# Cross attention on one core: the value mixes of two pairs of heads back to back in every second step, and four buffers of exponentials

## The chip, the cores and the metric

One NeuronCore of a Trainium2 chip runs one program: a decoder of four layers. The metric is the device time of one execution in microseconds (us), lower is better. TensorE (PE) multiplies; its weight loads (PEld) are separate instructions that run beside the matmuls. VectorE (DVE), ScalarE (ACT) and GpSimd (POOL) do the element work, SyncE (SP) issues the DMAs. Engines run their own instruction streams in order and wait for each other by semaphores.

## What is computed

The input x is 32 batches of 56 tokens with 128 features, the context is 32 batches of 1500 rows of 128. Each of four layers adds a self attention, a mixing with the context, and a feed forward part. In layers 1, 2 and 3 the mixing is a cross attention with 16 heads of 8 features:

```
Q = (query @ Wq + bq).reshape(B, Sq, H, D).transpose(0, 2, 1, 3)
K = (key @ Wk + bk).reshape(B, Sk, H, D).transpose(0, 2, 1, 3)
V = (value @ Wv + bv).reshape(B, Sk, H, D).transpose(0, 2, 1, 3)
scores = jnp.einsum('bhqd,bhkd->bhqk', Q, K) / jnp.sqrt(jnp.float32(D))
attn = jax.nn.softmax(scores, axis=-1)
out = jnp.einsum('bhqk,bhkd->bhqd', attn, V)
out = out.transpose(0, 2, 1, 3).reshape(B, Sq, E)
return out @ Wo + bo
```

Here query is the normalised x (56 rows a batch), key and value are both the context (1500 rows a batch).

## The kernel before

`cross_attention(chip, layer, scale)` is called three times. A call goes over the 32 batches, one batch to a *pass*; `all_passes` (L799) writes out the passes -2, -1, 0, then a hardware loop over seven groups of four passes, then the last four. Two heads make a *pair*: there are PR = 8 pairs a batch, and a pass has eight *steps*, one for each pair. Every engine has a `one_pass` of its own that fixes the order of its work by hand; semaphores tie them together.

What a pair needs, in the order in which it goes through the engines:

- `scores` (L907, matmuls L912): three matmuls, each 112 rows (two heads of 56 queries) by 500 keys, into the PSUM banks 0, 1 and 2. They run LEAD = 7 steps ahead of the rest. Bank n waits until VectorE has reduced bank n of the pair before (`topped`).
- `row_tops` (L1071, L1074): VectorE takes the largest score of each row, one reduction a bank. After four pairs, in step 4 and step 0, `split_tops` (L1076, five small operations, L1081 to L1089) splits the maxima in three bfloat16 parts. `turn_tops` (L918, L920) turns them on TensorE in steps 3 and 6; `place_first` (L1093) and `place_others` (L1097) put them beside the queries, so that the next product comes out with the maximum already taken off.
- `scores_by_key` (L922, L931): twelve matmuls give the same scores with the keys on the partitions, into the banks 3 to 5. They wait until ScalarE has emptied these banks of the pair before (`exp_done`).
- `exponentials` (L1014, L1016): one ScalarE instruction writes the exponentials of a pair to `probs_t`, of which there are two buffers.
- `mix_values` (L935, L943): the value mix, twelve fp32 products of 112 columns with 32 columns of weights (24 in the trace, since an fp32 product appears as two), on four column tiles in turn, added up in the bank MIX. It waits for the exponential of its pair. After four pairs `keep_mixed` (L1019, L1021) copies the bank away; `fold` (L948, L957) in step 3 of the next pass adds the four tiles up, and `keep_mix` (L1100) divides.

Beside these the pass makes the keys of the batch after next (`make_keys`, L891, steps 0, 1 and 2), which ScalarE copies (L1007), POOL splits (L1059 to L1065), and SP stacks by DMA; and the values of the next batch (`make_values`, L904, steps 4, 5 and 7; copy L1011).

TensorE's order in step s of a pass is: `scores_by_key` of pair s; keys, values, fold or turned tops where the step has them; `scores` of the pair seven steps ahead; `mix_values` of the pair s - 1. In step 0 that is pair 7 of the batch before.

Of the kernel before, what the change touches and what calls it, by code (L numbers as in the profile page):

```python
# [17 lines left out]
KC = 125  # L18
NC_ = NK // KC
# [732 lines left out]
PR = HX // 2  # L752
RW = 2 * S
# [8 lines left out]
VC = P // 32  # L762
VR = NC_ // VC
# [3 lines left out]
def cross_attention(chip, layer, scale):  # L767
# [9 lines left out]
    nc, ps, xn, x = chip.nc, chip.ps, chip.xn, chip.x  # L777
# [13 lines left out]
    TURNED, MIX, TURNS = 3, 6, 7  # L791
    KEY_STEPS, TURN_STEP, VALUE_STEPS, NEXT_TURN_STEP = (0, 1, 2), 3, (4, 5, 7), 6

    def wait(engine, semaphore, value):

        if not isinstance(value, int) or value > 0:
            engine.wait_ge(semaphore, value)
# [11 lines left out]
    def has(i):  # L809

        return not isinstance(i, int) or 0 <= i < B

    with ExitStack() as own:
        def sbuf(name, shape, dtype=F32):
            return own.enter_context(nc.sbuf_tensor(tag + name, shape, dtype))
# [12 lines left out]
        keys = [sbuf("keys%d" % u, [P, PR, NK], BF16) for u in range(2)]  # L828
        queries = [sbuf("queries%d" % u, [P, PR, RW], BF16) for u in range(2)]
        values = [sbuf("values%d" % u, [KC, NC_, VW]) for u in range(2)]  # L830
        probs_t = [sbuf("probs_t%d" % u, [KC, NC_, RW]) for u in range(2)]
        bank_top = sbuf("bank_top", [P, PR, NB_])
        top, top_left, top_parts = sbuf("top", [P, HP_]), sbuf("top_left", [P, HP_]), sbuf("top_parts", [P, 32], BF16)
        quarters = [sbuf("quarters%d" % u, [P, PR, 2, S]) for u in range(2)]
# [47 lines left out]
        def _(pe):  # L882
            def make_keys(i, o, n):
                if n == 0:
                    pe.wait_ge(ctx_landed[o % ROUND], 16 * ((i - o % ROUND) // ROUND) + 16 if isinstance(i, int) else 16 * ((i - o) // ROUND + o // ROUND) + 16)
                    if isinstance(i, int):
                        wait(pe, k_kept, NB_ * i)
                    wait(pe, v_kept, VR * (i - 1))
                else:
                    pe.wait_ge(k_kept, NB_ * i + n)  # L890
                nc.tensor.matmul(ps[:, TURNS, 0:KB], wk[:], ctx_t[o % ROUND][:, KB * n:KB * n + KB], start=True, stop=True).then_inc(k_done, 1)  # L891
# [30 lines left out]
            def scores_by_key(i, o, p):  # L922
                if p % HP_ == 0:
                    pe.wait_ge(first_placed, 2 * i + p // HP_ + 1)
                    if isinstance(i, int) and i == 0:
                        pe.wait_ge(both_filled, 16)
                if p % HP_ == 1:
                    pe.wait_ge(tops_placed, 2 * i + p // HP_ + 1)
                wait(pe, exp_done, PR * i + p)
                for c in range(NC_):  # L930
                    mm = nc.tensor.matmul(ps[0:KC, TURNED + c // VC, RW * (c % VC):RW * (c % VC) + RW],  # L931
                                          keys[o % 2][:, p, KC * c:KC * c + KC], queries[o % 2][:, p, :], start=True, stop=True)
                mm.then_inc(turned_done, 1)

            def mix_values(i, o, p):  # L935
                pe.wait_ge(exp_done, PR * i + p + 1)
                if p % HP_ == 0:
                    wait(pe, mixed_kept, 2 * i + p // HP_)
                if p == 0:
                    pe.wait_ge(v_kept, VR * i + VR)  # L940
                for c in range(NC_):
                    g = c % 4
                    mm = nc.tensor.matmul(ps[32 * g:32 * g + 32, MIX, RW * (p % HP_):RW * (p % HP_) + RW], values[o % 2][:, c, (PF + 1) * p:(PF + 1) * p + 32],  # L943
                                          probs_t[p % 2][:, c, :], start=(c < 4), stop=(c >= NC_ - 4))
                if p % HP_ == HP_ - 1:
                    mm.then_inc(mixed, 1)

# [19 lines left out]
            def one_pass(i, o):  # L967
                for step in range(PR):
                    if has(i):
                        scores_by_key(i, o, step)  # L970
                    if step in KEY_STEPS and has(i + 2):
                        make_keys(i + 2, o + 2, KEY_STEPS.index(step))
                    if step == TURN_STEP:
                        if has(i + 2):
                            pe.wait_ge(k_kept, NB_ * (i + 2) + NB_)
                        elif has(i + 1) or has(i):
                            pe.wait_ge(v_kept, VR * (i + 1))
                        if has(i - 1):
                            fold(i - 1, o - 1)
                        if has(i):  # L980
                            turn_tops(i, 1)
                    if step in VALUE_STEPS and has(i + 1):
                        if step == VALUE_STEPS[0] and has(i):
                            pe.wait_ge(first_placed, 2 * i + 2)
                            wait(pe, mix_kept, i)
                        make_values(i + 1, o + 1, VALUE_STEPS.index(step))
                    if step == NEXT_TURN_STEP and has(i + 1):
                        pe.wait_ge(v_kept, VR * (i + 1) + 2)
                        turn_tops(i + 1, 0)
                    ahead, pair = divmod(step + LEAD, PR)  # L990
                    if has(i + ahead):
                        scores(i + ahead, o + ahead, pair)
                    back, pair = divmod(step - 1, PR)
                    if has(i + back):
                        mix_values(i + back, o + back, pair)
            all_passes(pe, one_pass)
            for c in range(CH):
                pe.wait_ge(biased, c + 1)
                nc.tensor.matmul(ps[:, c, 0:CT], wo[:], mix[:, CB * c:CB * c + CB, :].rearrange("p b s -> p (b s)"),
                                 start=True, stop=True).then_inc(projected, 1)  # L1000

        @block.scalar
        def _(act):
            def keep_keys(i, n):
                act.wait_ge(k_done, NB_ * i + n + 1)
                wait(act, k_low, NB_ * (i - 1) + n + 1)
                nc.scalar.activation(key_whole[n][:], ps[:, TURNS, 0:KB], ACT.Identity, bias=bk[:, 0:1]).then_inc(k_kept, 1)  # L1007

            def keep_values(i, o, r):
                act.wait_ge(v_done, VR * i + r + 1)  # L1010
                nc.scalar.copy(values[o % 2][:, VC * r:VC * r + VC, 0:PR * (PF + 1)].rearrange("p c (j f) -> p c j f", f=PF + 1)[:, :, :, 0:PF],  # L1011
                               ps[0:KC, TURNS, :].rearrange("p (c j f) -> p c j f", c=VC, f=PF)).then_inc(v_kept, 1)

            def exponentials(i, p):  # L1014
                act.wait_ge(turned_done, PR * i + p + 1)
                nc.scalar.activation(probs_t[p % 2].rearrange("k (n c) r -> k n (c r)", c=VC), ps[0:KC, TURNED:TURNED + VR, 0:VC * RW],  # L1016
                                     ACT.Exp, scale=scale).then_inc(exp_done, 1)

            def keep_mixed(i, o, half):  # L1019
                act.wait_ge(mixed, 2 * i + half + 1)  # L1020
                nc.scalar.copy(quarters[o % 2][:, HP_ * half:HP_ * half + HP_].rearrange("p j c s -> p (j c s)"), ps[:, MIX, 0:HP_ * RW]).then_inc(mixed_kept, 1)  # L1021

            act.wait_ge(values_filled, 2)
            act.wait_ge(weights_landed, 11 * 16)
            for c in range(CH):
                act.wait_ge(q_kept, c + 1)
                for k in range(2):
                    nc.scalar.activation(query_parts[0][:, CB * c:CB * c + CB, k, :], q[:, c, :].rearrange("p (b s) -> p b s", s=S),
                                         ACT.Copy, scale=parity[:, k:k + 1]).then_inc(q_high, 1)
                for k in range(2):  # L1030
                    act.wait_ge(q_rest, 2 * c + k + 1)
                    nc.scalar.copy(query_parts[1][:, CB * c:CB * c + CB, k, :], q_left[k].rearrange("p (b s) -> p b s", s=S)).then_inc(q_mid, 1)

            def one_pass(i, o):
                for step in range(PR):
                    if step == 1 and has(i - 1):
                        keep_mixed(i - 1, o - 1, 1)
                    if step == 5 and has(i):
                        keep_mixed(i, o, 0)
                    if has(i):  # L1040
                        exponentials(i, step)
                    if step in KEY_STEPS and has(i + 2):
                        keep_keys(i + 2, KEY_STEPS.index(step))
                    if step in VALUE_STEPS and has(i + 1):
                        keep_values(i + 1, o + 1, VALUE_STEPS.index(step))
                if o == -2:
                    nc.scalar.copy(keys[1][TALL:P], spread(pair_rows[TALL:P, :], 2, NK)).then_inc(filled, 1)
            all_passes(act, one_pass)
# [1351 lines left out]
```

## Time and profile before

| | |
|---|---|
| median of three runs | 5160.35 us (5157.21 to 5160.76) |
| profiled execution: its run, its span | 5162.67 us, 5160.9 us |
| mean granted TensorE clock | 0.897 of full speed |
| PE busy with matmuls | 4142.6 us (80%) |
| PE busy with weight loads | 2790.2 us (54%) |
| DVE, ACT, POOL busy | 3131.7, 2156.6, 1472.0 us |
| L1074, maxima of the scores, DVE | 2304 times, 1412.2 us |
| L1016, exponentials, ACT | 768 times, 991.0 us |
| L931, scores by key, PE | 9216 matmuls, 702.7 us |
| L912, scores, PE | 2304 matmuls, 662.5 us |
| L943, value mix, PE | 18432 matmuls, 607.5 us |

The span is the time from the first to the last instruction of one profiled execution; the run's time has a little around it. Busy times of different engines overlap, and the ends of matmuls are modelled, so a PE that looks busy throughout need not be at its peak. In the timelines the distance from one weight load to the next tells better how TensorE went on. An idle time in brackets is that of the engine before the instruction, with what ended it; a wait for several semaphores is put down to the last one.

### The profile page before, as it was taken

To read this page: it belongs to the slowest core of one execution; us is meant where nothing else is said; L and a number is where in the kernel's file an instruction comes from. 1 tells how busy PE (TensorE), PEld (TensorE's weight loads), DVE (VectorE), ACT (ScalarE), POOL (GpSimd) and SP (SyncE) were. 2 spreads that over 40 slices of the span, in tenths; PEclk is the share of its full clock that TensorE was granted. 3 is DMA by queue.
4 is the path that set the end of the run, shared out by engine and by line. 5 is a ranking of instruction groups with operands and counts; after the bars stand their busy time and mean duration, and the time that the engine had idled before them with its cause. 6 is when DMAs were issued, how large, how long until landed. Compare 5 with 4: busy or idle time off the path is not lost. (4 is left out here: it accounts for less than half of the span.)

```text
span 5160.9 us, 124580 instructions
## 1 busy us (share of the span) xinstructions
PE 4142.6 (80%) x49374; PEld 2790.2 (54%) x49374; DVE 3131.7 (61%) x5441; ACT 2156.6 (42%) x2694; POOL 1472.0 (29%) x1222
## 2 busy tenths in 40 slices
PE   7955453999999696769999997957559999996398
PEld 5843321666666445636666674424226666664276
DVE  5621145877777454547777783347557777786543
ACT  2221243555555323335555553343344555554010
POOL 0000002555555000035555450003225555551000
PEclk9977776999999898979999998988779999998599
DMA  0035301555555140035555550100005555551265
GB/s 24 0 111 167 105 2 49 135 128 127 129 128 122 36 116 15 0 74 128 126 128 124 127 122 35 56 3 0 3 17 143 128 125 125 128 132 33 50 184 148
DMA packets 251672, 456.03 MB, mean 88 GB/s; under 512 B 135630, under 2 KB 143311, under 8 KB 251023
## 3 DMA queue, kind: packets, MB, share of 16 engines
q1 hardware_dynamic: 251246, 449.45, 34.2%
q8 instruction: 377, 6.18, 0.5%
q14 instruction: 49, 0.39, 0.0%
HBM read 207.56 MB, written 1.72 MB: 41 GB/s over the span
## 5 line engine op out<-in xcount | busy, mean ns | idle before, releaser
L1074 DVE TENSOR_REDUCE x_bank_top<-ps 112x1 f32<-112x500 f32 x2304 | 1412.2, 671 | 419.6 <-PE ps L912 410.1
L1016 ACT ACTIVATE x_probs_t<-ps 125x1344 f32<-125x1344 f32 x768 | 991.0, 1290 | 956.0 <-PE ps L931 956.0
L1059 POOL TENSOR_TENSOR x_key_part<-x_key_whole,x_nothing 128x500 bf16<-128x500 f32 x288 | 358.1, 1243 | 2526.8 <-ACT x_key_whole L1007 2526.8
L931 PE MATMUL ps<-x_queries,x_keys 128*125 128x112 bf16 x9216 | 702.7, 227 | 78.7 <-issue 67.6
L931 PEld LDWEIGHTS ps<-x_queries,x_keys 128*125 128x125 bf16 x9216 | 602.1, 140 | 215.1 <-issue 189.4
L912 PE MATMUL ps<-x_keys,x_queries 96*112 96x500 bf16 x2304 | 662.5, 390 | 47.2 <-DMA x_queries<-x_query_part 36.8
L943 PE MATMUL ps<-x_probs_t,x_values 125*32 125x112 f32 x18432 | 607.5, 265 | 3.6 <-ACT x_probs_t L1016 2.0
L943 PEld LDWEIGHTS ps<-x_probs_t,x_values 125*32 125x32 f32 x18432 | 420.5, 110 | 268.2 <-ACT x_probs_t L1016 180.3
L912 PEld LDWEIGHTS ps<-x_keys,x_queries 96*112 96x112 bf16 x2304 | 283.5, 133 | 342.2 <-DVE x_bank_top L1074 123.0
L891 PE MATMUL ps<-x_ctx_t,x_wk 128*128 128x500 f32 x576 | 336.0, 668 | 60.5 <-ACT x_key_whole L1007 58.1
L1063 POOL TENSOR_TENSOR x_key_part<-x_key_left,x_nothing 128x500 bf16<-128x500 f32 x288 | 359.9, 1250 | 22.6
L1065 POOL TENSOR_TENSOR x_key_part<-x_key_left,x_key_part 128x500 bf16<-128x500 f32 x288 | 327.2, 1136 | 22.6
L1061 POOL TENSOR_TENSOR x_key_left<-x_key_whole,x_key_part 128x500 f32<-128x500 f32 x288 | 326.5, 1134 | 22.6
L904 PE MATMUL ps<-x_wv,x_ctx_t 128*125 128x128 f32 x2304 | 318.4, 282 | 0.0
L904 PEld LDWEIGHTS ps<-x_wv,x_ctx_t 128*125 128x125 f32 x2304 | 277.3, 189 | 0.9 <-issue 0.6
L1279 PE MATMUL ps<-xn_lead,e_w 128*128 128x448 f32 x512 | 223.8, 543 | 3.2 <-DMA e_share<-m_weight_rows 3.2
L1007 ACT ACTIVATE x_key_whole<-ps,x_bk 128x500 f32<-128x500 f32 x288 | 193.6, 672 | 55.9 <-PE ps L891 55.8
L1306 ACT ACTIVATE e_silu<-ps 128x448 f32<-128x448 f32 x192 | 104.3, 543 | 247.8 <-PE ps L1279 247.8
L1285 PE MATMUL ps<-e_hidden,e_w 128*128 128x448 f32 x384 | 181.4, 554 | 9.1 <-DVE e_hidden L1324 5.0
L1011 ACT COPY x_values<-ps 125x512 f32<-125x512 f32 x288 | 168.1, 584 | 38.9 <-PE ps L904 38.9
L2164 POOL TENSOR_TENSOR g_k_diag<-g_kn,g_own_head 128x896 f32<-128x896 f32 x32 | 53.3, 1688 | 449.9 <-POOLq L1961 403.3
L458 PE MATMUL ps<-cm_ctx_n,cm_probs_t 125*64 125x128 f32 x768 | 78.7, 396 | 122.7 <-DMA cm_ctx_n<-in_ctx_n 122.7
(462 smaller groups left out, 5349.3 us busy)
## 6 DMA issues: line engine op xcount, KB each, us to landing
x_keys<-x_key_part SPq DMA_DIRECT2D x1152, 187.5 KB, 3.4
x_ctx_t<-in_ctx_t SPq DMA_DIRECT2D x96, 750.0 KB, 4.4
cm_ctx_t<-in_ctx_t SPq DMA_DIRECT2D x32, 750.0 KB, 12.9
cm_ctx_n<-in_ctx_n SPq DMA_DIRECT2D x32, 750.0 KB
x_queries<-x_query_part SPq DMA_DIRECT2D x1152, 14.0 KB, 2.3
e_share<-m_weight_scratch SPq DMA_DIRECT2D x32, 490.0 KB
e_spread_out<-m_slot_scratch SPq DMA_DIRECT2D x32, 490.0 KB
e_share<-m_weight_rows SPq DMA_DIRECT2D x32, 448.0 KB, 5.7
```

The lines of the kernel that those rows point to most:

```text
L891: nc.tensor.matmul(ps[:, TURNS, 0:KB], wk[:], ctx_t[o % ROUND][:, KB * n:KB * n + KB], start=True, stop=True).then_inc(k_done, 1)
L904: mm = nc.tensor.matmul(ps[0:KC, TURNS, P * c:P * c + P], ctx_t[o % ROUND][:, k0:k0 + KC], wv[:], start=True, stop=True)
L912: nc.tensor.matmul(ps[0:RW, n, 0:KB], queries[o % 2][0:TALL, p, :], keys[o % 2][0:TALL, p, KB * n:KB * n + KB], start=True, stop=True).the ...
L931: mm = nc.tensor.matmul(ps[0:KC, TURNED + c // VC, RW * (c % VC):RW * (c % VC) + RW], keys[o % 2][:, p, KC * c:KC * c + KC], queries[o % 2 ...
L943: mm = nc.tensor.matmul(ps[32 * g:32 * g + 32, MIX, RW * (p % HP_):RW * (p % HP_) + RW], values[o % 2][:, c, (PF + 1) * p:(PF + 1) * p + 3 ...
L1016: nc.scalar.activation(probs_t[p % 2].rearrange("k (n c) r -> k n (c r)", c=VC), ps[0:KC, TURNED:TURNED + VR, 0:VC * RW], ACT.Exp, scale=s ...
L1059: nc.gpsimd.tensor_tensor(part[0][:, cols], key_whole[n][:], nothing[:], ALU.add).then_inc(k_high, 1)
L1061: nc.gpsimd.tensor_tensor(key_left[:], key_whole[n][:], part[0][:, cols], ALU.subtract).then_inc(k_rest, 1)
L1063: nc.gpsimd.tensor_tensor(part[1][:, cols], key_left[:], nothing[:], ALU.add).then_inc(k_mid, 1)
L1065: nc.gpsimd.tensor_tensor(part[2][:, cols], key_left[:], part[1][:, cols], ALU.subtract).then_inc(k_low, 1)
L1074: nc.vector.tensor_reduce(bank_top[0:RW, p, n:n + 1], ps[0:RW, n, 0:KB], AX_X, ALU.max).then_inc(topped, 1)
L1279: mm = nc.tensor.matmul(ps[:, 4 + 2 * (n % 2) + m, 0:CT], w[u][:, s, m, :], tokens[c], start=True, stop=True)
```

## The change

There are four buffers `probs_t` in place of two, and the exponentials and the mixes choose theirs by p % 4. TensorE does no mix in an odd step any more. In an even step s it does those of the pairs s - 2 and s - 1, one after the other, at the place where it did that of pair s - 1; in step 0 these are pairs 6 and 7 of the batch before. Everything else, on all engines, stands as it was.

```diff
-        probs_t = [sbuf("probs_t%d" % u, [KC, NC_, RW]) for u in range(2)]
+        probs_t = [sbuf("probs_t%d" % u, [KC, NC_, RW]) for u in range(4)]
...
                     mm = nc.tensor.matmul(ps[32 * g:32 * g + 32, MIX, RW * (p % HP_):RW * (p % HP_) + RW], values[o % 2][:, c, (PF + 1) * p:(PF + 1) * p + 32],
-                                          probs_t[p % 2][:, c, :], start=(c < 4), stop=(c >= NC_ - 4))
+                                          probs_t[p % 4][:, c, :], start=(c < 4), stop=(c >= NC_ - 4))
...
                     if has(i + ahead):
                         scores(i + ahead, o + ahead, pair)
-                    back, pair = divmod(step - 1, PR)
-                    if has(i + back):
-                        mix_values(i + back, o + back, pair)
+                    for done in (step - 2, step - 1) if step % 2 == 0 else ():
+                        back, pair = divmod(done, PR)
+                        if has(i + back):
+                            mix_values(i + back, o + back, pair)
...
-                nc.scalar.activation(probs_t[p % 2].rearrange("k (n c) r -> k n (c r)", c=VC), ps[0:KC, TURNED:TURNED + VR, 0:VC * RW],
+                nc.scalar.activation(probs_t[p % 4].rearrange("k (n c) r -> k n (c r)", c=VC), ps[0:KC, TURNED:TURNED + VR, 0:VC * RW],
                                      ACT.Exp, scale=scale).then_inc(exp_done, 1)
```

## Rows read from the trace of the kernel before

**Rows 1.** Stretch 1000 to 1700: busy PE, PEld, DVE, ACT, POOL; clock, DMA share, GB/s.

```profile
1000.00:1700.00 700.00, 676.68 (x11077) 478.18 (x11080) 552.58 (x1086) 393.62 (x432) 369.53 (x312) 0.98 0.51 125
```

**Rows 2.** Timeline of PEld: start, length (us), instruction, shapes, count [idle before <-releaser].

```profile
1410.54 0.77 PEld L931 LDWEIGHTS ps<-x_queries,x_keys 128*125 128x125 bf16 x12 [0.17 <-issue]
...
1413.65 0.77 PEld L931 LDWEIGHTS ps<-x_queries,x_keys 128*125 128x125 bf16 x12 [0.17 <-issue]
...
1416.12 0.77 PEld L931 LDWEIGHTS ps<-x_queries,x_keys 128*125 128x125 bf16 x12 [0.17 <-ACT x_probs_t L1016]
...
1417.68 0.46 PEld L912 LDWEIGHTS ps<-x_keys,x_queries 96*112 96x112 bf16 x3
1418.52 0.54 PEld L943 LDWEIGHTS ps<-x_probs_t,x_values 125*32 125x32 f32 x24 [0.38 <-ACT x_probs_t L1016]
1419.23 0.77 PEld L931 LDWEIGHTS ps<-x_queries,x_keys 128*125 128x125 bf16 x12 [0.17 <-issue]
...
1425.39 0.77 PEld L931 LDWEIGHTS ps<-x_queries,x_keys 128*125 128x125 bf16 x12 [0.17 <-issue]
...
1427.73 0.13 PEld L912 LDWEIGHTS ps<-x_keys,x_queries 96*112 96x112 bf16 x1 [0.46 <-DVE x_bank_top L1074]
1428.08 0.54 PEld L943 LDWEIGHTS ps<-x_probs_t,x_values 125*32 125x32 f32 x24 [0.22 <-issue]
1428.79 0.77 PEld L931 LDWEIGHTS ps<-x_queries,x_keys 128*125 128x125 bf16 x12 [0.17 <-issue]
...
1434.20 0.13 PEld L912 LDWEIGHTS ps<-x_keys,x_queries 96*112 96x112 bf16 x1 [0.31 <-DVE x_bank_top L1074]
1434.55 0.54 PEld L943 LDWEIGHTS ps<-x_probs_t,x_values 125*32 125x32 f32 x24 [0.22 <-ACT x_probs_t L1016]
1435.26 0.77 PEld L931 LDWEIGHTS ps<-x_queries,x_keys 128*125 128x125 bf16 x12 [0.17 <-issue]
```

**Rows 3.** Timeline of DVE in the same stretch.

```profile
1412.36 0.16 DVE L1085 SCALAR_TENSOR_TENSOR x_top_left<-x_top,x_top_parts 112x4 f32<-112x4 f32 x1
...
1418.20 1.85 DVE L1074 TENSOR_REDUCE x_bank_top<-ps 112x1 f32<-112x500 f32 x3 [0.94 <-PE ps L912]
...
1423.58 1.01 DVE L1085 SCALAR_TENSOR_TENSOR x_top_left<-x_top,x_top_parts 112x4 f32<-112x4 f32 x1
...
1424.82 1.10 DVE L1089 TENSOR_TENSOR x_top_parts<-x_top_left,x_top_parts 112x4 bf16<-112x4 f32 x1
...
1430.73 0.28 DVE L1093 CAST x_queries<-ps 32x112 bf16<-32x112 f32 x1 [1.30 <-PE ps L920]
...
1432.30 3.72 DVE L1074 TENSOR_REDUCE x_bank_top<-ps 112x1 f32<-112x500 f32 x6
```

**Rows 4.** Timeline of PEld in a call's last pass.

```profile
1704.91 0.77 PEld L931 LDWEIGHTS ps<-x_queries,x_keys 128*125 128x125 bf16 x12 [0.91 <-ACT x_probs_t L1016]
...
1707.19 0.77 PEld L931 LDWEIGHTS ps<-x_queries,x_keys 128*125 128x125 bf16 x12 [0.91 <-ACT x_probs_t L1016]
1708.02 0.85 PEld L957 LDWEIGHTS ps<-x_quarters,x_place 128*32 128x32 f32 x64
1708.78 0.12 PEld L943 LDWEIGHTS ps<-x_probs_t,x_values 125*32 125x32 f32 x3
```

**Rows 5.** Timeline of PEld in a call's first pass, step 0 to 1, without a mix.

```profile
907.43 0.34 PEld L912 LDWEIGHTS ps<-x_keys,x_queries 96*112 96x112 bf16 x2 [0.29 <-issue]
908.06 0.77 PEld L931 LDWEIGHTS ps<-x_queries,x_keys 128*125 128x125 bf16 x12 [0.29 <-issue]
```

**Rows 6.** The page's costliest groups: busy us, mean ns | idle us, and what ended it.

```profile
L943 PEld LDWEIGHTS ps<-x_probs_t,x_values 125*32 125x32 f32 x18432 | 420.5, 110 | 268.2 <-ACT x_probs_t L1016 180.3
```

**Rows 7.** Timeline of PEld at a jump back of the loop, and the steps behind it.

```profile
1447.50 1.36 PEld L931 LDWEIGHTS ps<-x_queries,x_keys 128*125 128x125 bf16 x12 [3.71 <-issue]
...
1453.06 0.77 PEld L931 LDWEIGHTS ps<-x_queries,x_keys 128*125 128x125 bf16 x12 [0.17 <-issue]
...
1459.22 0.77 PEld L931 LDWEIGHTS ps<-x_queries,x_keys 128*125 128x125 bf16 x12 [0.17 <-issue]
```

## The prediction

> **What bounds the kernel now.** The page was read first: three stretches of the span, the three calls of `cross_attention`, hold nearly all of the costliest groups. The second view was the busy time in a long stretch of the first call: of 700 us the matmuls of TensorE (PE) fill 676.7, VectorE (DVE) is busy 552.6, ScalarE (ACT) 393.6, at a granted clock of 0.98 (nearly always the 2.4 GHz level) [rows 1]. That looks like a TensorE bound, but a matmul's end is modelled and an average hides single waits, so the third view was the order of PE's weight loads through one pass (one batch, eight steps), whose load to load distances are real issue times. A step is what lies between two starts of `scores_by_key` (SBK, L931).
>
> Step 5 takes 1413.65 - 1410.54 = 3.11, step 6 2.47, step 7 3.11, then steps 0 and 1 1425.39 - 1419.23 = 6.16 or 3.08 each, step 2 1428.79 - 1425.39 = 3.40, steps 3 and 4 together 1435.26 - 1428.79 = 6.47: 24.72 us for eight steps [rows 2]. Steps 0, 1 and 2 run the same instructions; 2 is 0.32 longer because its score matmuls (L912) are let go by DVE: the third bank's load, at 1427.73, ends an idle time put down to L1074, and so does the one of step 4 at 1434.20 [rows 2]. So PE sets the pace in most steps, but DVE's order fixes two stretches:
> - from SBK of step 0 to the mix of step 2: 1428.08 - 1419.23 = 8.85 [rows 2]. DVE reduces pair 7's scores, does the five small operations of `split_tops`, two of which last 1.01 and 1.10, then the reductions on which the score banks of step 2 wait [rows 3].
> - from SBK of step 3 to the mix of step 4: 1434.55 - 1428.79 = 5.76 [rows 2]. DVE stands idle for 1.30 until the turned tops arrive at 1430.73 (1.94 after SBK), and needs until 1432.30 for `place_first`, `keep_mix`, `place_others` before it reduces step 3's scores, whose third bank lets step 4's third bank go [rows 3].
>
> The exponential is a third limit: SBK writes the PSUM banks that ACT must have emptied. In the last pass, where PE has little else to do, SBK follows SBK after 1707.19 - 1704.91 = 2.28, waiting for L1016 [rows 4]. No step can be shorter.
>
> **The change, part by part.** Computation, instruction and DMA counts stay; nothing is moved past SP's or POOL's instructions. Per pass, the mix of pair p-1 leaves each odd step and goes behind the mix of pair p-2 in the next even step (the same even step that already holds one).
>
> What a mix costs alone. From the last score load (1417.68 + 0.46 - 0.13 = 1418.01) to the first mix load is 0.51, and from there to the next SBK 1419.23 - 1418.52 = 0.71 [rows 2]. Without a mix between, the same load to SBK is 908.06 - (907.43 + 0.34 - 0.13) = 0.42 [rows 5]. So a separate mix costs 0.51 + 0.71 - 0.42 = 0.80.
>
> What a second mix costs right behind another. No row shows it. Upper bound 0.80, no saving. Lower bound: the 24 loads of a mix begin within 0.54 - 0.11 = 0.43 [rows 2, 6], 0.45 for a whole block. I take 0.55: the entry and exit (0.80 - 0.55 = 0.25) are what is saved, the inner rate remains. The nearest row is the fold of the last pass, 64 fp32 matmuls on the same 32-column tiles, begun at 1708.02; the mix follows it at 1708.78, 0.76 later, with no idle time given [rows 4], so two such blocks join without a seam. Were nothing else in the way, four pairs per pass would save 4 x 0.25 = 1.0 us.
>
> The second wait is free: both mixes wait for exponentials that SBK of the same step has already waited for (for step - 1). Without four buffers the exponential of an even step would overwrite what the delayed mix still reads; with them ACT gets no new wait. `keep_mixed` still follows the end of step 0 and step 4, `fold` comes two steps later. Their instructions are covered as before. The key stacks' DMAs depend on SBK, which moves by at most about one microsecond within a pass; cost taken as nothing, and it would show as PE idle before L912 put down to x_queries.
>
> Now where the time goes, by the fixed stretches:
> - Steps 0 to 2. Step 0 gains a mix (+0.55), step 1 loses one (-0.80, to 2.28, just at the exponential's floor). But the mix of step 2 can't start before 8.85, which DVE fixes from the scores of step 0, and these aren't moved. PE only waits longer for the third bank. Then two mixes: 8.85 + 0.71 + 0.55 = 10.11 against 9.56, +0.55.
> - Steps 3 and 4. Step 3 loses its mix, but 5.76 from SBK to the mix of step 4 is again DVE's. 5.76 + 1.26 = 7.02 against 6.47, +0.55.
> - Steps 5 and 6. PE alone: 3.11 - 0.80 = 2.31 and 2.47 + 0.55 = 3.02, 5.33. DVE: its reductions of a step like 5 (values made, as in step 7) begin 1418.20 - 1416.12 = 2.08 after SBK and last 1.85 [rows 2, 3]; the load of step 6's third bank follows 0.05 later and the mix 1434.55 - 1434.20 = 0.35 after it [rows 2]; 2.08 + 1.85 + 0.05 + 0.35 + 1.26 = 5.59. The later one counts: 5.59 against 5.58, no change.
> - Step 7 has neither a wait for DVE nor a second mix: 3.11 - 0.80 = 2.31, just above the floor 2.28: -0.80.
>
> Sum per pass 0.55 + 0.55 + 0.01 - 0.80 = +0.3. What is late next is thus DVE's chain: its two long detours used to run while PE did a mix in steps 1 and 3, and now PE idles there, and the mixes that were cover stand between DVE and its next scores.
>
> There are 3 calls with 32 batches; the last batch of a call has no scores beyond its step 0 and is left at no change, so 93 passes x 0.3 = +27.9. At 18 jumps back of the loop over four passes (6 a call) PE is idle for 3.71 and restarts cold: the loads of its first SBK last 1.36 in place of 0.77 [rows 2, 7]. In the passes behind them step 2 has no wait for DVE (1459.22 - 1453.06 = 6.16 = 2 x 3.08 [rows 7]), so steps 0 to 2 gain only 0.55 - 0.80 + 0.55 = +0.30 in place of +0.55: -0.25 x 18 = -4.5. The odd step in front of the jump loses its mix like any step 7 (in the sum). When the jump's idle time starts to count isn't shown: from PE's last matmul, then it is unchanged; if the sequencer runs ahead, some 0.5 less or more each, +-9 in all, for the range.
>
> Sum: +27.9 - 4.5 = +23.4, with about 1 us for step 0 of the last passes +24.5. The profiled execution's span is 5160.9 (5162.67 its run), the median of the three 5160.35; they agree within 0.05%. Forecast 5160.35 + 24.5 = 5185.
>
> **The rivals.**
> (A) The second mix saves nothing, 0.80. Steps 0-2, 3-4 and 5-6 each get 0.25 more: 93 x 0.75 = +70, 5255. Against: the seamless fold and mix [rows 4]. The Trainium skill (TensorE: Matmul & The Clock Gate, Part 3, The mechanism) says that weight loads overlap running matmuls only where their row groups differ; all mixes use the same rows, so by that rule joining them would gain nothing. The trace disagrees with it: 24 loads of 110 ns begin within 0.43 [rows 2, 6].
> (B, the other side) DVE's split finishes sooner. The same operation L1085 takes 0.16 at step 4 and 1.01 at step 0, and L1089 1.10 [rows 3]: they end with a POOL operation. If POOL's phase against DVE moves so that these two don't fall upon it, 1.8 us go, step 2 no longer waits, and steps 0 to 2 take 3.63 + 2.28 + 3.63 = 9.54, -0.02 in place of +0.55. The pass is then 0.27 shorter than before: 93 x -0.27 = -25, 5135. It decides from the point where the split ends 0.3 sooner in most passes. Against: key 0 that starts POOL and the scores that start the split both come from step 0, before the added mix.
> (C) PE bound throughout, the full saving: 24.72 - 0.32 - 1.00 = 23.40, 93 x -1.32 = -123, 5037. For: PE 676.7 of 700 busy [rows 1]. Against: 8.85 and 5.76 would both have to shrink. The skill (Perfetto Trace Analysis, Identifying the Most-Contended Engine) compares VectorE's occupancy with TensorE's weight loads, not its matmuls: here 552.6 against 478.2 of 700 [rows 1], which puts DVE ahead. By that rule relieving PE gains nothing.
> (D) The terms cancel: the jumps come out 0.5 to 1 us cheaper each (-9 to -18) and a pass costs 0.2: about 5165, no difference.
>
> **How the numbers follow.** Forecast 0.62, of it 0.54 more than 0.2% slower and 0.08 within; A 0.08; B 0.12; C 0.06; D 0.12. Slower by over 0.2% (10 us, about what a measurement of this kernel can tell from no change): 0.54 + 0.08 = 0.62; within: 0.20; faster: 0.18. The forecast's own range is 5165 to 5210 (second mix 0.45 to 0.65, jumps +-9). The whole range leaves out C and the upper end of A, and takes in B: 5130 to 5235.
>
> **What would show it.** In the profile after: a pass of about 25.0 where it was 24.72; two mix blocks of 48 loads in even steps, the second 0.55 long; SBK to SBK about 3.63, 2.28, 4.2, 2.5, 4.5, 2.3, 3.3, 2.3 from step 0 on; PE idle before the third score load of steps 2, 4 and 6 put down to L1074, more than before; the distances 8.85 and 5.76 unchanged; L1016 still 1.29. The prediction is wrong if 8.85 or 5.76 shrink (B, C), if the second mix takes 0.8 (A), or if the idle time at the jumps moves by over 1 us.

## The result and the profile after

The changed kernel takes 5198.57 us in the median of four runs (5192.12 to 5206.64), the kernel before 5160.56 (5157.21 to 5160.95): ratio 1.0076, 95% interval 1.0058 to 1.0093. It is slower by about 38 us. The profiled executions have spans of 5190.3 and 5160.9, 29.4 apart: that of the changed kernel took 5192.12, 6 us under its median, that of the kernel before 5162.67, 2 us over the median.

The first view is the same long stretch of the first call as in [rows 1], busy time of PE, PEld, DVE, ACT, POOL, then clock, DMA share, GB/s:

```profile
1000.00:1700.00 700.00, 667.85 (x10917) 484.54 (x10917) 532.61 (x1066) 386.51 (x425) 369.53 (x312) 0.97 0.51 125
```

PE's matmuls are busy for less of it, and so is DVE: both now stand idle more. The costliest groups say where (busy us, mean ns | idle time before, and what ended most of it); first the kernel before, with three that ended it, then the changed one, with the first alone, as its page has it:

```profile
L912 PEld LDWEIGHTS ps<-x_keys,x_queries 96*112 96x112 bf16 x2304 | 283.5, 133 | 342.2 <-DVE x_bank_top L1074 123.0 <-issue 112.1 <-DMA x_queries<-x_query_part 43.7
```

```profile
L912 PEld LDWEIGHTS ps<-x_keys,x_queries 96*112 96x112 bf16 x2304 | 290.8, 132 | 464.4 <-DVE x_bank_top L1075 284.9
L943 PEld LDWEIGHTS ps<-x_probs_t,x_values 125*32 125x32 f32 x18432 | 435.8, 111 | 107.0 <-issue 74.8
```

The mix loads have lost idle time (107.0 against 268.2 in [rows 6]). The saving of the joined mixes is in it, but not all of it is saved: some of the waiting now stands in front of other loads. The score loads have gained idle time: 284.9 us end with a VectorE reduction, where it was 123.0. The DMAs of the queries end 42.6 us of it in the changed kernel's trace where they ended 43.7, so the transfers cost nothing, as forecast. Lines behind L993 are one higher in the changed kernel, so L1074 is L1075 there.

The third view is the timeline of PEld through one pass, the counterpart of [rows 2]:

```profile
1401.74 0.77 PEld L931 LDWEIGHTS ps<-x_queries,x_keys 128*125 128x125 bf16 x12 [0.33 <-issue]
...
1404.11 1.12 PEld L943 LDWEIGHTS ps<-x_probs_t,x_values 125*32 125x32 f32 x48 [0.38 <-ACT x_probs_t L1017]
1405.39 0.77 PEld L931 LDWEIGHTS ps<-x_queries,x_keys 128*125 128x125 bf16 x12 [0.17 <-issue]
...
1407.67 0.77 PEld L931 LDWEIGHTS ps<-x_queries,x_keys 128*125 128x125 bf16 x12 [0.29 <-ACT x_probs_t L1017]
...
1410.23 0.13 PEld L912 LDWEIGHTS ps<-x_keys,x_queries 96*112 96x112 bf16 x1 [0.46 <-DVE x_bank_top L1075]
1410.58 1.12 PEld L943 LDWEIGHTS ps<-x_probs_t,x_values 125*32 125x32 f32 x48 [0.22 <-issue]
1411.87 0.77 PEld L931 LDWEIGHTS ps<-x_queries,x_keys 128*125 128x125 bf16 x12 [0.17 <-issue]
...
1417.61 1.12 PEld L943 LDWEIGHTS ps<-x_probs_t,x_values 125*32 125x32 f32 x48 [0.22 <-issue]
1418.90 0.77 PEld L931 LDWEIGHTS ps<-x_queries,x_keys 128*125 128x125 bf16 x12 [0.17 <-issue]
...
1422.88 0.13 PEld L912 LDWEIGHTS ps<-x_keys,x_queries 96*112 96x112 bf16 x1 [0.46 <-DVE x_bank_top L1075]
1423.23 1.12 PEld L943 LDWEIGHTS ps<-x_probs_t,x_values 125*32 125x32 f32 x48 [0.22 <-issue]
1424.52 0.77 PEld L931 LDWEIGHTS ps<-x_queries,x_keys 128*125 128x125 bf16 x12 [0.17 <-issue]
...
1426.86 0.77 PEld L931 LDWEIGHTS ps<-x_queries,x_keys 128*125 128x125 bf16 x12 [0.32 <-issue]
```

The first row is step 0, and the last step 0 of the next pass: 1426.86 - 1401.74 = 25.12 where it was 24.72. From SBK of step 0 to the mixes of step 2 it is 1410.58 - 1401.74 = 8.84, from SBK of step 3 to the mixes of step 4 1417.61 - 1411.87 = 5.74: the two distances that VectorE sets are the 8.85 and 5.76 of before. Behind each now stand two mixes, 1411.87 - 1410.58 = 1.29, where one took 0.71. Steps 5 and 6 take 1424.52 - 1418.90 = 5.62, and step 6's third score load waits for DVE. Step 7 takes 2.34.

And the timeline of DVE in the same pass, the counterpart of [rows 3]:

```profile
1406.08 1.01 DVE L1086 SCALAR_TENSOR_TENSOR x_top_left<-x_top,x_top_parts 112x4 f32<-112x4 f32 x1
...
1407.33 1.09 DVE L1090 TENSOR_TENSOR x_top_parts<-x_top_left,x_top_parts 112x4 bf16<-112x4 f32 x1
1408.34 3.59 DVE L1075 TENSOR_REDUCE x_bank_top<-ps 112x1 f32<-112x500 f32 x6
1413.80 0.28 DVE L1094 CAST x_queries<-ps 32x112 bf16<-32x112 f32 x1 [1.86 <-PE ps L920]
...
1415.36 3.60 DVE L1075 TENSOR_REDUCE x_bank_top<-ps 112x1 f32<-112x500 f32 x6
```

DVE idles 1.86 in front of the turned tops where it idled 1.30. The 0.56 more is the second mix of step 2, which PE does while DVE has nothing. The split's two long operations are still there, so rival B didn't happen.

### The profile page after: what moved, and what is told of

Read it like the earlier page. It is cut to its first block and busy times, and to the rows that moved or that the text cites. A ratio compares the mean times of both kernels' runs of the same rounds, so it can differ in the third digit from the quotient of the medians.

```text
span 5190.3 us, 124601 instructions
## 1 busy us (share of the span) xinstructions
PE 4136.8 (80%) x49374; PEld 2825.1 (54%) x49374; DVE 3093.9 (60%) x5441; ACT 2157.8 (42%) x2694; POOL 1472.6 (28%) x1222
## 5 line engine op out<-in xcount | busy, mean ns | idle before, releaser
L1075 DVE TENSOR_REDUCE x_bank_top<-ps 112x1 f32<-112x500 f32 x2304 | 1402.3, 670 | 437.7 <-PE ps L912 431.5
L912 PE MATMUL ps<-x_keys,x_queries 96*112 96x500 bf16 x2304 | 733.3, 397 | 91.9 <-DVE x_bank_top L1075 46.4
L931 PE MATMUL ps<-x_queries,x_keys 128*125 128x112 bf16 x9216 | 690.7, 225 | 76.7 <-issue 61.9
L912 PEld LDWEIGHTS ps<-x_keys,x_queries 96*112 96x112 bf16 x2304 | 290.8, 132 | 464.4 <-DVE x_bank_top L1075 284.9
L943 PE MATMUL ps<-x_probs_t,x_values 125*32 125x112 f32 x18432 | 529.5, 263 | 2.0 <-ACT x_probs_t L1017 2.0
L943 PEld LDWEIGHTS ps<-x_probs_t,x_values 125*32 125x32 f32 x18432 | 435.8, 111 | 107.0 <-issue 74.8
L1022 ACT COPY x_quarters<-ps 128x448 f32<-128x448 f32 x192 | 102.2, 532 | 300.4 <-PE ps L943 300.4
```

The source lines that it names most:

```text
L912: nc.tensor.matmul(ps[0:RW, n, 0:KB], queries[o % 2][0:TALL, p, :], keys[o % 2][0:TALL, p, KB * n:KB * n + KB], start=True, stop=True).the ...
L1075: nc.vector.tensor_reduce(bank_top[0:RW, p, n:n + 1], ps[0:RW, n, 0:KB], AX_X, ALU.max).then_inc(topped, 1)
```

## The experiments

They ask what the two traces alone can't say: whether the loss goes when VectorE's chain is cut or the mixes stand elsewhere, and what is left of it when the loop's jumps are taken away. In the table, pass is the commonest distance between two exponentials of step 0, good to 0.01; excess is what the first 31 such distances of each of the three calls have over 31 passes, summed. Most of it lies at the loop's jumps, but a single long pass anywhere counts as well. Both are worked out from the starts of L1016 (or its line in the other kernels) in each kernel's profile.

| kernel | pass, us | excess, us (calls 1, 2, 3) | median, us | ratio to before (95%) |
|---|---|---|---|---|
| before | 24.72 | 98 (28, 39, 31) | 5160.56 | 1 |
| changed | 25.13 | 89 (28, 19, 42) | 5198.57 | 1.0076 (1.0058 to 1.0093) |
| buffers_only | 24.72 | 103 | 5169.32 | 0.9996 (0.9982 to 1.0009) |
| odd_steps | 24.57 | 113 (36, 31, 47) | 5177.19 | 1.0021 (1.0008 to 1.0033) |
| steps_1356 | 24.23 | 106 | 5133.28 | 0.9938 (0.9921 to 0.9954) |
| steps_0356 | 23.66 | 107 | 5084.27 | 0.9842 (0.9825 to 0.9858) |
| short_before | 24.40 | 99 | 5145.66 | 0.9947 (0.992 to 0.9974) |
| short_after | 24.59 | 114 | 5167.9 | 1.0004 (0.9989 to 1.002) |
| unroll_before | 24.66 | -8 | 5054.25 | 0.9793 (0.9776 to 0.9809) |
| unroll_after | 25.02 | -5 | 5092.07 | 0.9856 (0.9838 to 0.9875) |
| waits_ahead | 25.13 | 80 (40, 20, 20) | 5193.55 | 1.006 (1.0039 to 1.008) |
| steps_0356_unrolled | 23.63 | 1 | 4975.75 | 0.9622 (0.9598 to 0.9646) |

Each ratio goes with runs of the kernel before on the same chip, whose medians lay between 5160.6 and 5172.3; medians of different rows of the table can differ by that.

**Only the buffers.** The changed kernel with the old mixes:

```diff
-                    for done in (step - 2, step - 1) if step % 2 == 0 else ():
-                        back, pair = divmod(done, PR)
-                        if has(i + back):
-                            mix_values(i + back, o + back, pair)
+                    back, pair = divmod(step - 1, PR)
+                    if has(i + back):
+                        mix_values(i + back, o + back, pair)
```

> Four buffers of exponentials, the mixes one to a step as in the kernel before. Theory (VectorE's chain fixes two stretches of a pass, and the added mixes stand behind them): the buffers alone do nothing, 5160 within 5. Rival (the buffers, by their place in memory or by letting ScalarE run ahead, cost something themselves): 5175 to 5200.

0.9996: the buffers by themselves show no cost and no gain (the interval is 0.9982 to 1.0009), and the kernel's pass is that of before step by step. The loss lies in the order of the mixes.

**VectorE's chain cut short.** In both kernels `split_tops` ends after its second operation, so the second and third parts of the maxima are left out:

```diff
-                nc.vector.tensor_scalar(top_parts[0:RW, 0:HP_], top[0:RW, :], -1.0, None, ALU.mult).then_inc(tops_chain, 1)
...
+                nc.vector.tensor_scalar(top_parts[0:RW, 0:HP_], top[0:RW, :], -1.0, None, ALU.mult).then_inc(tops_split, 1)
```

> The kernel before with a short split of the maxima: only the first bfloat16 part is made, three of the five small VectorE operations are left out (so the maxima are rounded, part of the computation is left out). It takes about 2.3 us from VectorE's chain in steps 0 to 2. Theory: step 2 loses its 0.32 wait in 75 passes, the rest is TensorE's own time: 5160 - 24 = 5136. Rival (VectorE's chain isn't what lets step 2 go): 5160.

> The changed kernel with the same short split (the second and third parts of the maxima are left out). Theory: steps 0 to 2 come down from 10.13 to TensorE's own 3.66 + 2.28 + 3.66 = 9.60 in 75 passes, the stretch of steps 3 and 4 keeps its wait: 5198 - 40 = 5158, so the distance to the kernel before with the short split shrinks from 38 to about 22. Rival (the loss comes from the joined mixes or the code's place, not from VectorE's chain): the distance stays 38.

The passes are 24.40 and 24.59, to 0.01 what was expected (24.72 - 0.32; 25.13 - 0.53). The distance between the two kernels falls from 0.41 to 0.19 a pass. This is the changed kernel so cut, PEld from step 0 to step 3:

```profile
1396.50 0.77 PEld L931 LDWEIGHTS ps<-x_queries,x_keys 128*125 128x125 bf16 x12 [0.33 <-issue]
...
1400.15 0.77 PEld L931 LDWEIGHTS ps<-x_queries,x_keys 128*125 128x125 bf16 x12 [0.17 <-issue]
...
1402.43 0.77 PEld L931 LDWEIGHTS ps<-x_queries,x_keys 128*125 128x125 bf16 x12 [0.29 <-ACT x_probs_t L1017]
...
1404.80 1.12 PEld L943 LDWEIGHTS ps<-x_probs_t,x_values 125*32 125x32 f32 x48 [0.38 <-ACT x_probs_t L1017]
1406.09 0.77 PEld L931 LDWEIGHTS ps<-x_queries,x_keys 128*125 128x125 bf16 x12 [0.17 <-issue]
...
1411.48 0.13 PEld L912 LDWEIGHTS ps<-x_keys,x_queries 96*112 96x112 bf16 x1 [0.46 <-DVE x_bank_top L1075]
```

The mixes of step 2 begin 1404.80 - 1396.50 = 8.30 after SBK of step 0, no longer 8.84, and steps 0 to 2 take 9.59, the same as 3.08 + 3.08 + 3.40 of before to 0.03. In step 4 PE waits for DVE as ever: that chain wasn't touched. In time, the ratios stand 1.0004 - 0.9947 = 0.0057, some 29 us, apart, where 22 were expected and 39 (0.0076) is the uncut distance; the intervals (about 0.002 and 0.003 each side) exclude neither 22 nor 39, and the excess is 15 us higher in the changed one of the two. The step times carry this verdict; the medians don't decide it.

**The same joined mixes elsewhere.** Three kernels with the list of mixes of each step written out; `keep_mixed` goes to step 2 (odd_steps, steps_1356) and step 6 (all three). The list of the changed kernel would be {0: (-2, -1), 2: (0, 1), 4: (2, 3), 6: (4, 5)}; a negative number is a pair of the batch before.

```diff
+MIXES = {1: (-2, -1), 3: (0, 1), 5: (2, 3), 7: (4, 5)}
...
-                    for done in (step - 2, step - 1) if step % 2 == 0 else ():
+                    for done in MIXES.get(step, ()):
...
-                    if step == 1 and has(i - 1):
+                    if step == 2 and has(i - 1):
...
-                    if step == 5 and has(i):
+                    if step == 6 and has(i):
```

> The same four joined pairs of mixes, but in the odd steps: pairs 6 and 7 of the batch before in step 1, then 0 and 1 in step 3, 2 and 3 in step 5, 4 and 5 in step 7; the copies of the mixed bank go one ScalarE step later. Theory: no mix stands behind VectorE's chain any more. Steps 0 to 2 end 8.76 after their start (third score load at 8.50, 0.26 to the next step) instead of 9.56; steps 3 and 4 take 3.84 + 2.31 = 6.15 instead of 6.47 (TensorE's own work); steps 5, 6, 7 take 3.66, 2.28 (the exponential's floor), 3.66 instead of 8.69. Pass 24.5 against 24.72 before and 25.13 of the changed kernel: 93 x -0.2 = -19, about 5142. Rival (joining the mixes costs by itself, wherever they stand): as the changed kernel, 5190 to 5205.

> Joined pairs of mixes in steps 1, 3, 5 and 6 (6 and 7 of the batch before; 0, 1; 2, 3; 4, 5). Theory: as with the odd steps, but step 6 carries a pair that fits under TensorE's own work and step 7 is short: 8.76 + 6.15 + 3.66 + 3.02 + 2.34 = 23.93, 93 x -0.79 = -73, about 5087. Rival (joining costs by itself): 5190 or more.

> Mixes where VectorE's chain leaves room: pairs 5, 6, 7 of the batch before in step 0, then 0 and 1 in step 3, 2 and 3 in step 5, 4 in step 6. Theory: steps 0 to 2 4.2 + 2.28 + 2.28 = 8.76, as long as VectorE needs anyway; steps 3 and 4 6.15; 3.66, 2.47 and 2.34 for 5 to 7: 23.4, 93 x -1.34 = -125, about 5036. Rival (joining costs by itself): 5190 or more. Between: if VectorE, busy 21.4 of 23.4, becomes the bound, 24 to 24.5 a pass, 5095 to 5140.

Joining doesn't cost by itself. With the same four pairs in the odd steps the pass falls from 25.13 to 24.57 (24.5 expected). The time didn't follow as far: 1.0021 where 0.9965 was expected. By the profile the pass gives 93 x 0.15 = 14 and the excess takes 15 (113 against 98), so that the gain is gone; the 11 us above the kernel before (1.0021) are not in these passes, and where they lie stays open. This kernel is a miss in time with its passes as expected.

steps_1356 is the second miss: 24.23 a pass, 23.93 expected. Its step 6 takes 3.29 in the pass shown, not 3.02. DVE and POOL there:

```profile
1277.51 1.08 DVE L1085 TENSOR_SCALAR x_top_parts<-x_top 112x4 bf16<-112x4 f32 x1
...
1279.12 1.85 DVE L1076 TENSOR_REDUCE x_bank_top<-ps 112x1 f32<-112x500 f32 x3
```

```profile
1277.42 1.14 POOL L1067 TENSOR_TENSOR x_key_part<-x_key_left,x_key_part 128x500 bf16<-128x500 f32 x1
```

```profile
1281.02 0.13 PEld L913 LDWEIGHTS ps<-x_keys,x_queries 96*112 96x112 bf16 x1 [0.46 <-DVE x_bank_top L1076]
```

A DVE operation on four columns, 0.17 elsewhere, lasts 1.08 and ends at 1278.59, 0.03 behind a POOL operation that ends at 1278.56; the reductions after it come late, and step 6's third bank with them. I had counted PE's own work alone for that step. The passes of the same trace bear it out: in 21 of the 93 this operation is short, and step 6 takes 3.04 or 3.05 in 19 of these; in the other 72 its middle value is 3.28. The Trainium skill (SBUF — State Buffer, SBUF: two separate sides) says that VectorE and GpSimd share a pair of ports as an exclusive lock, which a VectorE operation needs in a 2-port mode or with two SBUF inputs (the latter only against a GpSimd operation that reads SBUF), and that the one that comes second is held for the whole instruction of the other. The trace agrees in the times, here and in the long operations of [rows 3]; which mode an operation ran in it doesn't show.

steps_0356 is the fastest with the loop, 0.9842. Its PEld from step 0 on:

```profile
1395.39 0.77 PEld L932 LDWEIGHTS ps<-x_queries,x_keys 128*125 128x125 bf16 x12 [0.33 <-issue]
...
1397.76 1.69 PEld L944 LDWEIGHTS ps<-x_probs_t,x_values 125*32 125x32 f32 x72 [0.38 <-ACT x_probs_t L1018]
1399.62 0.77 PEld L932 LDWEIGHTS ps<-x_queries,x_keys 128*125 128x125 bf16 x12 [0.17 <-issue]
...
1404.18 0.77 PEld L932 LDWEIGHTS ps<-x_queries,x_keys 128*125 128x125 bf16 x12 [0.18 <-ACT x_probs_t L1018]
...
1415.63 0.13 PEld L913 LDWEIGHTS ps<-x_keys,x_queries 96*112 96x112 bf16 x1 [0.40 <-DVE x_bank_top L1076]
```

Steps 0 to 2 take 1404.18 - 1395.39 = 8.79 with three mixes in them, where the changed kernel needs 10.13: the mixes now lie beside VectorE's detour. The pass is 23.66, 0.26 above the expected 23.4 (0.15 of it in step 6, for the same reason as above: 2.47 as expected in 21 of the 22 passes with the short operation, 2.63 as the middle value of the others). About 5036 was expected and 0.9842, some 81 us under before, measured.

**Without the jumps.** The loop over groups of four passes is written out, in the kernel before and in the changed one:

```diff
-        for i in (-2, -1, 0):
-            one_pass(i, i)
-        with engine.Fori(0, (B - 4) // ROUND) as j:
-            for o in range(1, ROUND + 1):
-                one_pass(ROUND * j + o, o)
-        for i in range(B - 3, B + 1):
+        for i in range(-2, B + 1):
             one_pass(i, i)
```

> The kernel before with the passes of the three cross attentions written out, no loop and no jump back. Theory: the 18 jumps cost about 5.3 us each (idle time, then the 1.2 GHz level), they go: 5160 - 95 = 5065. Rival (instructions must be fetched all the same and cost the same in line): 5160.

> The changed kernel with the passes written out. Theory: what is left of the difference is that of the pass, 25.13 - 24.72 = 0.41, 93 x 0.41 = 38 over the kernel before written out: about 5103. Rival (a good part of the loss lies at the jumps): 10 to 25 over it.

The two lie 5092.07 - 5054.25 = 37.8 apart, the full loss of the change; the passes, 0.36 apart, give 93 x 0.36 = 33. So the loss belongs to the passes and doesn't need the jumps. Both passes are a little shorter than with the loop, by 0.06 and 0.11, nearly all of it in step 4; why I didn't follow up. By the ratios the loop costs the kernel before 2.1% (107 us) and the changed one 2.2% (113 us).

**What a jump costs.** In the changed kernel, the third call, PE's loads at a jump:

```profile
4141.41 0.60 PEld L931 LDWEIGHTS ps<-x_queries,x_keys 128*125 128x125 bf16 x5 [3.58 <-issue]
4144.27 0.82 PEld L931 LDWEIGHTS ps<-x_queries,x_keys 128*125 128x125 bf16 x7 [2.26 <-issue]
```

PE comes back after 3.58, does five loads, and stands idle again for 2.26, in the middle of SBK. It does so at all six jumps of this call (2.26 to 2.79). In the first call of the same kernel the twelve loads come in one piece, and a smaller second idle time stands before the scores, at all six jumps (1.04 to 2.05); in the second call there is none:

```profile
1454.71 1.35 PEld L931 LDWEIGHTS ps<-x_queries,x_keys 128*125 128x125 bf16 x12 [3.05 <-issue]
...
1457.67 0.46 PEld L912 LDWEIGHTS ps<-x_keys,x_queries 96*112 96x112 bf16 x3 [1.18 <-issue]
```

The experiment moves the code by a few instructions:

```diff
-            pe.wait_ge(q_kept, CH)
+            for _ in range(10):
+                pe.wait_ge(q_kept, CH)
```

> The changed kernel with nine more waits for a semaphore that is already there, once a call, ahead of TensorE's first pass: 5 more TensorE instructions a call, so everything behind them lies 5, 10 and 15 instructions later. Theory (what a jump back costs hangs on where its target lies in the instruction stream): the pass stays at 25.13, the sum of what the three calls take beyond 31 such passes moves by more than 5 us in at least one call, up or down; the whole 5185 to 5210. Rival (the jump's cost belongs to the order of the work): the calls' excess stays within 2 us of 28, 19 and 42.

The third call's excess falls from 42 to 20, the first call's rises from 28 to 40, the pass stays 25.13. In the rows the second idle time has left the third call (first row); in the first call it has grown and come forward, from the scores to between SBK and the keys (the other two), 1.76 to 2.39 at its six jumps:

```profile
4147.31 0.77 PEld L931 LDWEIGHTS ps<-x_queries,x_keys 128*125 128x125 bf16 x12 [3.25 <-issue]
...
1460.16 0.77 PEld L931 LDWEIGHTS ps<-x_queries,x_keys 128*125 128x125 bf16 x12 [3.44 <-issue]
1463.32 0.50 PEld L891 LDWEIGHTS ps<-x_ctx_t,x_wk 128*128 128x128 f32 x2 [2.39 <-issue]
```

So where the second idle time falls, and whether there is one, hangs on where the code lies. It isn't chance: short_after, with the changed kernel's TensorE code, has it at the same two places, and buffers_only, with that of the kernel before, repeats its calls within 4 us (32, 39, 32 against 28, 39, 31). But the place of TensorE's code isn't all: short_after's excess is 36, 32, 47 where the changed kernel has 28, 19, 42, partly by first idle times that are some 0.5 longer. That PE waits there for its instructions is my reading; the profile says only "issue". In the medians this kernel and the changed one are alike (1.006 and 1.0076).

**Both gains.** steps_0356 written out as above:

> Mixes in steps 0, 3, 5 and 6 (three, two, two, one), and the passes written out without a loop. The two gains add if they are independent: 5054 of the kernel before written out, less 93 x (24.66 - 23.62) = 97, about 4957. Rival (VectorE's chain takes part of it once the jumps no longer give it time to catch up): 4970 to 4990.

4975.75 in the median, 0.9622 of the kernel before: 3.8%, or 195 us less. It is 19 us above the sum of the two, within the rival's 4970 to 4990. The commonest pass is as expected, 23.63, so VectorE's chain takes nothing from that one; the single passes that last 0.2 to 0.6 longer are part of the 19 (excess 1 against -8), and which of them wait for what I didn't follow up. Whether it is the rival's mechanism is thus not shown.

## Why the prediction was right

5185 was forecast, in a range of 5130 to 5235, with 0.62 for slower by over 0.2%. It is 5198.57, and slower, for the reason given; the sizes of two terms were off, and the part on the jumps failed. Point by point:

- **The two fixed stretches.** 8.85 and 5.76 were to stay; they are 8.84 and 5.74. The steps were forecast as 3.63, 2.28, 4.2, 2.5, 4.5, 2.3, 3.3, 2.3; they are, from exponential to exponential and as the middle value of all passes, 3.66, 2.28, 4.19, 2.43, 4.60, 2.28, 3.34, 2.34. The cut kernels show that the first stretch is VectorE's, and the moved mixes that it matters what stands behind it. The second stretch was not cut; that VectorE sets it rests on the rows.
- **The second mix** was to cost 0.55, between 0.45 and 0.80; it costs 1.29 - 0.71 = 0.58. This is the term that was too small, and the lower bound of 0.43 was no bound for it: the loads start in fours, each four 0.096 behind the last, and a mix is six fours, so the next mix's first load comes 6 x 0.096 = 0.58 behind its own first, while the 0.43 reached only to the start of the last load. It counts three times in a pass (steps 2, 4 and 6, of which each stretch carries one). The second, smaller one: a mix taken out of a step with values saves 3.11 - 2.34 = 0.77, not 0.80, since the way from the scores to SBK is longer there than in the first pass's row that I used [rows 5]. By the rows the stretches come to +0.57 (steps 0 to 2), +0.56 (3 and 4) and +0.04 (5 and 6), and step 7 to -0.77: 0.40 a pass (0.41 by the exponentials) where 0.3 was forecast, 38 us for 93 passes where it was 28.
- **Steps 5 and 6.** 5.59 forecast, 5.62 measured, with DVE letting the third bank go, as the sum said.
- **The jumps.** This part was wrong, by the prediction's own sign (an idle time at the jumps that moves by over 1 us): in the second call it fell from between 4.57 and 4.71 to between 2.58 and 3.22, and in the first and third a second one of 1.0 to 2.8 came in. I had -4.5 for the passes behind the jumps and +-9 for the gap. The excess fell by 10 us in the profiled execution, but by +0, -20 and +11 in the three calls. The order of the mixes is the same in all three, so it alone doesn't decide this; waits_ahead, with the same order, moves the calls by +12, +1 and -22. The total stayed near the +-9 by luck; its reason (when the gap begins to count) wasn't the one that decides. In the profiles 38 for the passes less 10 make the 28 to 29 us between the spans. The timed medians are 38 apart; the other 9 us are what the two profiled executions lie off their medians (6 and 2 us), and in which part of the program they fall I can't say.
- **Rivals.** A (0.80 for the second mix) and C (a PE bound throughout) are excluded by the rows; C would have needed both stretches to shrink. B didn't occur by itself, but the cut kernels are its mechanism made by hand, and its arithmetic held: steps 0 to 2 at 9.59 where 9.54 was worked out. D is excluded by the interval.

## What to carry to other kernels

An engine that looks busy throughout can still be led by another in parts of its cycle; look for the loads whose idle time another engine ends, and measure from there to the work behind them. Work that is moved to save a switch must not land behind such a wait: the same four joins cost 0.41 a pass in the even steps, save 0.15 in the odd ones, and save 1.06 where they fill the time in which VectorE has its detour. A loop's jump is a cost of its own, here some 6 us each (107 and 113 us for 18), and it can change when code ahead of it does, so two versions of a looped kernel are best compared by their passes, or written out.

## What the runs showed of the hardware

- Weight loads of 32 columns and fp32 matmuls join without a seam over two and three pairs: 24 loads in 0.54, 48 in 1.12, 72 in 1.69 us. They go in fours, one to each column tile: 7 ns from load to load within a four, 96 ns from one four to the next. A mix by itself costs some 0.2 us more than one joined to another (0.80 against 0.58).
- A jump back over a long loop body leaves TensorE idle for 2.6 to 3.6 us in the changed kernel, in two of the calls with a second gap of 1.0 to 2.8 within the next 3 us; a few more instructions ahead of the loop (5, 10 and 15 in the three calls, by my count) took that second gap out of the third call and brought it forward in the first. Without loop and jumps the granted clock is 1.00 over the long stretch, where it is 0.97 with them. Here is the changed kernel written out:

```profile
1000.00:1700.00 700.00, 677.95 (x11506) 495.90 (x11507) 551.94 (x1103) 405.66 (x444) 368.86 (x312) 1.00 0.51 125
```

- A small VectorE operation can be held by a GpSimd operation until 0.02 to 0.03 us behind its end, and then lasts up to 1.15 us in place of 0.17. Only some are: in the kernel before the operations of L1083, L1085, L1087 and L1089 are held, while the reduction of L1081 (0.17) and the bf16 copy of L1097 (0.32) last the same whether a GpSimd operation is under way or not.
